# Two cross-attentions whose normalised input is turned by transposing DMAs instead of by TensorE

## The reference

```python
x = x + tanh(g_xattn[0]) * attention0(layernorm(x), ctx, 16 heads of 32)
x = x + tanh(g_ffn[0])   * bit_ffn(layernorm(x))          # 8-bit activations, ternary weights, a convolution
x = x + tanh(g_xattn[1]) * attention1(layernorm(x), ctx, mask, 8 heads of 64)
x = x + tanh(g_ffn[1])   * fp4_ffn(layernorm(x))          # blocks of 16 rounded to FP4, weights too

# attention: q = h @ Wq; k = ctx @ Wk; v = ctx @ Wv; softmax(q k^T * scale) v @ Wo
```

## Time and profile before

| | |
|---|---|
| time, median of 3 runs | 2118.52 us (2117.62 to 2121.26) |
| profiled execution | 2128.36 us, its span 2126.5 us |
| mean granted TensorE clock | 0.94 |
| busy: TensorE | 1841.5 us (87%), weight loads 1278.3 (60%) |
| busy: DVE, GpSimd, ACT | 1423.4 (67%), 1244.9 (59%), 993.9 us (47%) |
| DMA engines, mean share and rate | 39.4% in the kernel's queue, 105 GB/s |

### The profile page before, as it was taken

The page is one execution under the profiler, slowest core; times in us unless marked ns, Lnnn a source line. Parts: engine busy times, 40 slices in busy tenths (PEclk is TensorE's granted clock), DMA queues, the critical chain, the costliest instruction groups (busy, mean ns, idle before and its releaser), DMA issues. The chain is left out here.

```text
span 2126.5 us, 41085 instructions
## 1 busy us (share of the span) xinstructions
PE 1841.5 (87%) x14610; PEld 1278.3 (60%) x14610; DVE 1423.4 (67%) x2597; ACT 993.9 (47%) x1276; POOL 1244.9 (59%) x1465
## 2 busy tenths in 40 slices
PE   5799999999997469997578999999999967899995
PEld 3477677777776357785346666666666653344442
DVE  4777777776765368885444666766767544899862
ACT  3176667766668597773223434434434341111110
POOL 3176766766766434443303766767667434989963
PEclk9899999999998579999889999999999988999997
DMA  7445445445430411111632444544545543234332
GB/s 205 112 109 131 114 114 133 118 114 128 115 92 27 173 30 51 36 43 44 204 88 74 138 121 131 144 131 117 142 119 146 133 86 90 63 72 95 72 71 57
DMA packets 271258, 222.41 MB, mean 105 GB/s; under 512 B 150008, under 2 KB 239864, under 8 KB 270584
## 3 DMA queue, kind: packets, MB, share of 16 engines
q1 hardware_dynamic: 271096, 220.22, 39.4%
HBM read 129.96 MB, written 67.53 MB: 93 GB/s over the span
## 5 line engine op out<-in xcount | busy, mean ns | idle before, releaser
L739 POOL TENSOR_TENSOR a_p_hl<-a_p,a_p_hl 125x448 bf16<-125x448 f32 x540 | 563.4, 1045 | 459.4 <-ACT a_p_hl L905 430.6
L895 ACT ACTIVATE a_p<-a_psum 125x1344 f32<-125x1344 f32 x192 | 247.8, 1291 | 134.9 <-PE a_psum L1348 127.8
L1079 DVE TENSOR_REDUCE a_nm<-a_psum 112x1 f32<-112x750 f32 x256 | 237.3, 933 | 103.6 <-PE a_psum L1368 102.7
L905 ACT ACTIVATE a_p_hl<-a_p 125x1344 bf16<-125x1344 f32 x192 | 253.9, 1323 | 102.5 <-PE a_psum L1386 98.9
L1386 PEld LDWEIGHTS a_psum<-a_v_st,a_p_hl 125*128 125x128 bf16 x4608 | 180.2, 99 | 50.0 <-issue 30.5
L1386 PE MATMUL a_psum<-a_v_st,a_p_hl 125*128 125x65 bf16 (+2 forms) x4608 | 192.0, 196 | 20.7 <-POOL a_p_hl L739 16.9
L1258 PE MATMUL a_psum<-a_chl,a_w 128*128 128x375 bf16 x768 | 142.7, 332 | 23.2 <-DVE a_w L969 15.3
L1258 PE MATMUL a_psum<-a_chl,kept_w 128*128 128x375 bf16 x768 | 138.4, 333 | 21.0 <-DVE kept_w L969 18.2
L1368 PE MATMUL a_psum<-a_k_st,a_q_st 96*112 96x375 bf16 x512 | 128.0, 337 | 29.7 <-DVE a_nm L1079 20.1
L1368 PE MATMUL a_psum<-kept_k,a_q_st 128*112 128x375 bf16 (+1 forms) x512 | 122.7, 339 | 32.1 <-DVE a_nm L1074 15.3
L1258 PE MATMUL a_psum<-a_w,a_chl 128*125 128x512 bf16 x576 | 138.8, 383 | 8.6 <-DVE a_m_parts L1060 5.7
(11 more groups left out here) (263 smaller groups left out, 3884.9 us busy)
## 6 DMA issues: line engine op xcount, KB each, us to landing
a_k<-a_k_tmp SPq DMA_DIRECT2D x64, 375.0 KB, 3.1
a_k_st<-a_k SPq DMA_DIRECT2D x96, 187.5 KB, 3.4
kept_k<-a_k SPq DMA_DIRECT2D x96, 187.5 KB, 3.4
a_c<-in_ctx_t SPq DMA_DIRECT2D x16, 750.0 KB, 5.9
ctx_parts<-a_chl SPq DMA_DIRECT2D x16, 750.0 KB, 9.9
a_chl<-ctx_parts SPq DMA_DIRECT2D x16, 750.0 KB, 5.6
a_q_st<-a_q SPq DMA_DIRECT2D x192, 56.0 KB, 2.2
parts<-a_fhl SPq DMA_DIRECT2D x24, 352.0 KB, 3.8
```

Of the source, the lines that this page charges most:

```text
L739: ins = nc.gpsimd.tensor_tensor(p_hl[0:MC, h % 2, 1, cols], p32[0:MC, h % 2, cols], p_hl[0:MC, h % 2, 0, cols], ALU.subtract)
L895: nc.scalar.activation(p32[0:MC, par, :].rearrange("p (b n) -> p b n", b=3), st[0:MC, :, 0:2 * S], ACT.Exp, scale=scale).then_inc(exp_done, 1)
L905: nc.scalar.activation(p_hl[0:MC, par, 0, :], p32[0:MC, par, :], ACT.Copy).then_inc(phi_done, 1)
L1079: ins = nc.vector.tensor_reduce(out, sm_[0:HALF, 0:2, 0:MK], AX.XY, ALU.max, negate=True)
```

## The change

- A unit X has no matmuls and no PSUM bank. ACT copies half k of xn to bf16 (`input_high`), DVE subtracts it (`input_low`), both from and to SBUF, and SyncE turns high and low half together into xnT with one transposing DMA (`turn_input`), 112 by 1,024 bf16. Q(0) on TensorE waits for both DMAs. The slots are as before.
- The halves lie in a buffer of their own in a0, and in a1 in that of the residual and the output (xo), with waits for it.
- Tile 0's steps in a1's last row: its load and moments in quarter 0, GpSimd's root at the end of quarter 0, scaling and GpSimd's rounding in quarter 1, ACT's half at the end of quarter 2, DVE's at the end of quarter 3. Its transposing DMAs stay where they are.
- The split of a rounded weight piece in quarter 3 moves from the first head to the second, ahead of the powers.

```diff
+        xb_own = sb("xb", [HALF, 2, 2, D], BF16) if stacked else None
+        xb = xb_own if stacked else xo[:, :, :].bitcast(BF16).rearrange("p s (a d) -> p s a d", a=2)
...
+            def turn_input(b, k):
+                n_low = value(b.index * 2 + k + 1)
+                sp.wait_ge(x_low, n_low)
+                settle()
+                sp.dma_start(xnT[:, :, :, k * HALF:(k + 1) * HALF].rearrange("p a c s -> p (a c) s"),
+                             xb[:, k, :, :].rearrange("p a d -> p (a d)"), transpose=True).then_inc(xT_in, 16)
+
             def load_residual(b):
+                if not stacked and (b + 2).exists():
+                    sp.wait_ge(xT_in, (b.number + 3) * 32)
...
-                if q == 2 and b.number == B - 1 and kept:
+                if q == 0 and b.number == B - 1 and kept:
                     sp.wait_ge(f_split, FP4_PIECES)
...
-                if kept and b.number == B - 1 and q == 2:
-                    first_tile()
+                if kept and b.number == B - 1 and q == 0:
+                    first_root_steps()
+                if kept and b.number == B - 1 and q == 1:
+                    first_round()
...
+            def input_high(b, k):
+                act.wait_ge(xn_ready, b.index * 2 + k + 1)
+                if b.number != 0:
+                    act.wait_ge(xT_in, b.index * 32)
+                if not stacked and (b.number is None or b.number >= 2):
+                    act.wait_ge(out_sent, b.index * 32 - 63)
+                nc.scalar.activation(xb[:, k, 0, :], xn[:, k, :], ACT.Copy).then_inc(x_high, 1)
...
-                if kept and q == 3 and b.number == B - 1:
+                if kept and q == 2 and b.number == B - 1:
                     act.wait_ge(first_rounded, 1)
...
+            def input_low(b, k):
+                dve.wait_ge(x_high, b.index * 2 + k + 1)
+                nc.vector.tensor_tensor(xb[:, k, 1, :], xn[:, k, :], xb[:, k, 0, :], ALU.subtract).then_inc(x_low, 1)
...
-                    if m >= 1:
-                        split_weights(m - 1)
+                if at == (3 if q == 3 else 1) and m >= 1:
+                    split_weights(m - 1)
...
-                if at == (2, 0):
+                if at == (0, 1):
                     dve.wait_ge(first_in, 16)
-                if at == (3, 0):
+                if at == (1, 1):
                     dve.wait_ge(first_root, 1)
-                if at == (0, 0):
+                if at == (3, 1):
                     dve.wait_ge(first_high, 1)
...
-                if kind == "X":
-                    pe.wait_ge(xn_ready, b.index * 2 + k + 1)
+                if unit[:2] == ("Q", 0):
+                    pe.wait_ge(xT_in, (b.index + 1) * 32)
...
-                if (unit[:2] == ("OP", 0) and not (stacked and (b + 2).exists())
-                        or unit[:2] == ("Q", 0) and not stacked and (b.number is None or b.number >= 2)):
+                if unit[:2] == ("OP", 0) and not (stacked and (b + 2).exists()):
                     pe.wait_ge(unit_done, n - 1)
...
-                elif kind == "X":
-                    for c in range(KC):
-                        ins = nc.tensor.transpose(bank[:, c * HALF:(c + 1) * HALF], xn[:, k, c * P:(c + 1) * P],
-                                                  ident[0:HALF, 0:HALF])
```

More of the change, by code:

```diff
@@ L299, in cross_attention @@
         out_sent = sem("out_sent")
+        x_high, x_low, xT_in = sem("x_high"), sem("x_low"), sem("xT_in")
         k_sent, q_sent = sem("k_sent"), sem("q_sent")
@@ L321, in cross_attention @@
         mid = Item(3, 1)
-        UBODY = sum(len(quarter_units(q, b)) for q, b in ((2, mid), (3, mid), (0, mid + 1), (1, mid + 1)))
+        UBODY = sum(sum(u[0] != "X" for u in quarter_units(q, b)) for q, b in ((2, mid), (3, mid), (0, mid + 1), (1, mid + 1)))
         PAIRS = (B - 2) // 2
@@ L529, in after_unit @@
                 kind, k, b = unit
+                if kind == "X":
+                    turn_input(b, k)
+                    return None
                 n = units.next()
@@ L767, in first_tile, with first_round @@
                 ins.then_inc(first_root, 1)
+            def first_round():
                 pool.wait_ge(first_scaled, 1)
@@ L848, in mask_bias_t @@
                                          bias=-MASKED).then_inc(mask_ready, 1)
+            def input_high(b, k):
[5 more added lines that the diff above has]
+                nc.scalar.activation(xb[:, k, 0, :], xn[:, k, :], ACT.Copy).then_inc(x_high, 1)
             def unit_hi_part(unit):
                 kind, k, b = unit
+                if kind == "X":
+                    input_high(b, k)
+                    return
                 n = units.next()
@@ L871, in unit_hi_part @@
                                                bank[0:MC, :].rearrange("p (h d) -> p h d", h=H), ACT.Copy)
-                elif kind == "X":
-                    ins = nc.scalar.activation(xnT[:, 0, :, k * HALF:(k + 1) * HALF],
-                                               bank[:, 0:KC * HALF].rearrange("p (c s) -> p c s", c=KC), ACT.Copy)
                 elif kind == "M":
@@ L1021, in split_chunk @@
                     ins.then_inc(ctx_split, 1)
+            def input_low(b, k):
+                dve.wait_ge(x_high, b.index * 2 + k + 1)
+                nc.vector.tensor_tensor(xb[:, k, 1, :], xn[:, k, :], xb[:, k, 0, :], ALU.subtract).then_inc(x_low, 1)
             def unit_lo_part(unit):
                 kind, k, b = unit
+                if kind == "X":
+                    input_low(b, k)
+                    return
                 n = units.next()
@@ L1045, in unit_lo_part @@
                                                   v_st[0:MC, b.parity, k, :, 0:DK], ALU.subtract)
[L1046 to L1050, removed]
                 elif kind == "OT":
@@ L1216, in quarter @@
                     weight_step(q, b, 2 * j + 1)
-                    if kept and (b.number == B - 1 and q in (2, 3) or b.number == B and q == 0):
+                    if kept and b.number == B - 1:
                         first_tile((q, j))
@@ L1264, in place_products @@
                 for unit in quarter_units(q, b):
+                    if unit[0] == "X":
+                        continue
                     first, last = PLACES[q][unit[:2]]
```

3 lines of the change are left out of this document (1 added, 2 removed).

## The result

The changed kernel takes 2180.8 us (median of 4 runs, 2176.0 to 2185.4) against 2118.4 us for the kernel before. The ratio is 1.028, with a 95% interval of 1.026 to 1.030: slower, as forecast (2170, range 2128 to 2198). The profiled execution has a span of 2174.7 us, 48.2 more than before. It is one of the faster executions of its kernel, and that of before one of the slower, so the two traces show 48 of the 62 us.

The account below looks back on a forecast made before the run. TensorE's instruction stream was taken to bound both attentions. First attention 26.4, second 27, prologues 5 and seam -7 gave +51 us, on the median of 2118.5 a forecast of 2170 us, range 2128 to 2198.

Parts of the forecast that it names:

- TensorE sets the time, and a wait put into its stream costs its length: Both attentions: work taken off TensorE is worth its length, a wait put in costs nearly its length.
- Q0 late by the queue: Q0's transposing DMAs wait behind large context transfers: Q0 4.4 us late in the first attention, 4.0 in the second.
- the first attention's term: Six rows of the first attention: 6 x (4.4 + 1.0 - 1.0) = 26.4 us.
- The clock: TensorE runs slower after each new stall at Q0: 1.0 us each, with 0 and 1.7 as the ends.
- Won back: Part of TensorE's own waits vanishes while it stands: 1.0 us a row in the first attention, 0.5 in the second.
- The later split, taken at nothing: Quarter 3 of the second attention: delays GpSimd's rounding and the store behind it, 0, at most 1 us a row.
- Prologues: Row 0's Q0 late behind the weight loads: 2.5 us for each attention, 5 in all, bounds 0 and 5 each.
- The seam: Second attention to last stage: tile 0's earlier steps shorten a chain of waits, 7 us gained.
- B: Rival: context transfers don't hold the transposes up, only 3.1 us from issue counts; +25, 2144 us; chance 0.25.
- C: Rival: faster, Q0's stall takes the place of later waits in the row; about -8, 2110 us; chance 0.11.
- D: Rival: clock stays lower longer (1.7), K regroup late, nothing won back, prologues 9, seam gives 2; +78, 2196; chance 0.07.

Follow-up runs that it names:

- e12_spare: e1_seam with a0's new input path also run beside TensorE's, into a buffer nobody reads: 2107.0 us, ratio 0.993 to the kernel before.
- e5_ctx: Changed kernel with a0's save of the split context and a1's load of the context's second half issued behind X(1)'s turn: 2162.5 us, ratio 1.018.
- e1_seam: Changed kernel with both attentions' inputs turned by TensorE again, leaving tile 0's earlier steps and the later split: 2102.9 us, ratio 0.990.
- e8_split: Kernel before with only the later split of a weight piece in quarter 3: 2110.5 us, ratio 0.993.
- e9_pro: Changed kernel with X units sooner in both attentions, a0's save behind them, and rows 0 and 1 turned by TensorE: 2140.5 us, ratio 1.009.
- e11_three: e9_pro with a1's load of the context's first half also issued behind the turns: 2134.0 us, ratio 1.005.
- e13_apart: e11_three with a0's X1 back in its old slot behind V5: 2133.1 us, ratio 1.005.

## Why the prediction was right, and where not

**TensorE sets the time, and a wait put into its stream costs its length.** Right. e12_spare shows the converse: the same work without the wait costs at most some 7 us.

**Q0 late by the queue.** Right in kind, shown by e5_ctx. In size, the first attention's term was right by luck. In its five rows Q0 starts 45.4 us after the row's output transposes instead of 40.7, so it is 4.6 us late, and I took 4.4. But the wait at Q0 is only 2.6 us in these rows, and 1.2 of that is time that the transposes freed. Most of the rest stands ahead of Q0: the wait for the maxima, 1.1 us longer, and the lower clock behind it, some 1.9 us. DVE's subtraction of X0 now stands ahead of these maxima for 1.28 us (at 414.15), where the old one took 0.61. In e12_spare, with the same subtractions and the transposes still on TensorE, this wait is 1.06 us. The prediction had nothing for it.

I had also put both transfers in full behind the end of the full stretch. In the trace the share is at 0.99 from 414 us on, and the first turn is issued at 417.14, so it will have moved inside that stretch; no run tests this. In the second attention I took 4.0 us late, and in its five rows Q0 is 4.5 us late (55.7 us behind the output's transposes instead of 51.2); TensorE, without its transposes, was to stand some 5, and it stood 5.4 on average.

**The clock.** 1.0 us was taken after each stall. In a1, busy time per row went from 81.5 to 81.9 us though 1.2 us of transposes had gone: 1.6 us. The rows before had lost some clock behind their regroup waits; against e1_seam (80.7, clock 1.00) it is 2.4. In a0 busy time went from 75.4 to 75.1, which gives 0.9 us by the same reckoning: 1.9 lost ahead of Q0, behind the wait for the maxima, and 1.0 regained behind Q0. The two levels show in Q0's twelve matmuls, 2.42 against 1.31 us.

**Won back.** For a0 I took 1.0 us a row. From Q0 to the next output it took 36.7 us instead of 39.1, so 2.4 came back: the waits for K's low part and its regroup fell from 2.2 to 1.0 us, and the clock is at 1.00 there instead of 0.98. That is why the row grew by 2.2 us only. For a1 I took 0.5. In its five rows: 5.7 of wait, plus 1.6 of clock, less 1.2 of transposes, is 6.1; the row grew by 4.4, so 1.7 came back. But this is no catching up. It is the later split: against e1_seam the same sum is 5.7 + 2.4 - 1.2 = 6.9 for a growth of 6.5, and 0.4 came back.

**The later split, taken at nothing.** This is the step that failed. I looked only at what it makes later (GpSimd's rounding) and priced it 0 to +1 us a row. I did not look at what had stood behind it on DVE: K's low part, the regroup and the 2.0 us wait on that in the earlier trace rows. I had read that wait as moving with TensorE. By itself the edit is worth 15 us (e8_split), and it hides inside the change: against e1_seam, a row of a1 grew from 82.6 to 89.1, 6.5 us and not 4.4. The forecast's 4.5 met the measured 4.4 with two errors of opposite sign, the lower clock and the split.

**Prologues.** Taken at 2.5 each; row 0's Q0 is 5.0 us late, at the upper bound, and in a1 4.7 (12.4 us after the stage's first matmul instead of 7.7). My row for "TensorE idle in any case" was the time behind Q0; with Q0 late, the K unit that waited there for the context follows it. That e9_pro gains 0.004 agrees with some 8 us for both.

**The seam.** -7 forecast; -5.9 by landmarks, and 4.8 between e8_split and e1_seam.

**The sum.** +51 forecast on the profiled execution, +48.2 in the traces, +62 by the medians. The right total rests partly on luck: 26 forecast for the rows of a0 and some 13 measured (6 x 2.2), 5 for the prologues and some 10 measured, and a split that offset a dearer second attention. Of the rivals, B (the queue doesn't matter) fell with e5_ctx, C (the waits come back) with the row lengths, though in a0 2.4 us a row did come back. Of D, the dearer clock showed in a1 (it had 1.7 us) and so did the prologues (it had 9), but no late regroup: the scores of a1 waited 0.6 us a row for K, 0.4 in e1_seam.

**A transpose on TensorE or by DMA.** The Trainium skill, page "VectorE: DVE Perf Modes", section "The three transpose paths", advises TensorE for a transpose whose result may be in PSUM. This case agrees: four blocks took 0.6 us there, and no turn landed in under 2.9 us. That transposing DMAs are as fast as regular ones (the Trainium skill, page "Advanced Engine Details and Errata", section "X-Bar Transpose (TRN2)") no run here tests: no turn ran alone, and a landing holds more than the transfer.

**What stays open.** e11_three still loses 0.016 to e1_seam, some 33 us. The traces show 25 of them: 15 in a1, of which the context waits (12.1) would account for most, 8 in a0 and 2 in the last stage. The code of a0 is the same in e9_pro, where a0 took 739.0 us, as in e1_seam, and the last section shows what differs. e1_seam's trace is 8.6 us above its median, which is as much as the traces leave out; where these 8 us lie is open. The best version is e1_seam, the change without its transposing DMAs: 0.990 of the time of the kernel before.

## What to carry to other kernels

Work moved off the bounding engine onto a DMA pays only if its consumer has slack for issue, queue and landing; look for the large transfers that the same queue has just been given, and for what already has no slack behind the consumer. When an instruction is moved later on a busy engine, list what stood behind it there as well as what waits for it: the gain may lie in the queue. And when several edits come together, time each alone, since a right total may hide a gain that one should keep.

## What was unexpected of the hardware

The issue of a transposing DMA on SyncE lasts 1.24 us when the queue is free, as the prediction had it. With large transfers ahead it lasted up to 2.57 us in a0 and 3.19 in a1; in e5_ctx, with less ahead, the median is back at 1.3. The issuing engine itself is held up, and so is whatever it issues next.

A stall of TensorE as short as 2.5 us can take the clock with it, or not. In the changed kernel even 1.49 us did: over the 6 us behind that wait the granted clock was 0.72 in four of the six rows of a0 and 1.00 in two. Behind the waits of 1.06 to 1.09 us in the same place in e12_spare and e13_apart it was 1.00 in all twelve. In e9_pro and e11_three the first attention has the same code and the same six stalls of 2.53 us. Here are the 6 us behind each stall of rows 5 to 7, in e9_pro:

```profile
401.26:407.26 6.00, 6.00 (x50) 4.37 (x51) 3.62 (x8) 3.32 (x4) 3.56 (x4) 0.72 0.90 198
481.98:487.98 6.00, 6.00 (x66) 4.88 (x67) 5.11 (x11) 4.73 (x6) 5.76 (x5) 1.00 0.87 191
562.01:568.01 6.00, 6.00 (x50) 4.31 (x51) 3.61 (x8) 3.06 (x4) 3.56 (x4) 0.72 1.00 188
```

and in e11_three:

```profile
403.78:409.78 6.00, 6.00 (x44) 4.31 (x45) 3.22 (x8) 2.91 (x4) 3.56 (x4) 0.54 0.88 196
485.40:491.40 6.00, 6.00 (x43) 4.28 (x44) 3.22 (x8) 2.92 (x4) 3.56 (x4) 0.51 1.06 196
567.37:573.37 6.00, 6.00 (x43) 4.29 (x44) 3.22 (x8) 2.92 (x4) 3.56 (x4) 0.52 1.01 188
```

The granted clock is 1.00, 0.72 or some 0.52 after one and the same stall. Over all six rows the missing clock is 5.0 us in e9_pro (three rows at 0.72 or 0.73) and 11.9 us in e11_three (two at 0.72, three at 0.51 to 0.54): 7 of the 8 us between the two. So what a stall costs here is its own length and then between nothing and 3 us more, and one profiled run can't tell which.
